# Partial sums of exponentials split between VectorE and GpSimd in the masked cross attentions of a two-layer Perceiver-like block

## The reference

```python
attn = jnp.einsum('bihd,bjhd->bhij', q, k)                 # 512 queries x 8192 keys, 16 heads
attn = jnp.where(padding_mask[:, None, None, :], attn, -jnp.inf)
p = jax.nn.softmax(attn, axis=-1)
ctx = jnp.einsum('bhij,bjhd->bihd', p, v).reshape(b, s1, c)
out = ctx @ Wo.T + bo
```

## Time and profile before

| | us |
|---|---|
| median of 2 runs | 1712.45 (1708.62 to 1716.28) |
| span of the profiled execution | 1710.0 |
| second half of L0x, first to last exponential | about 284 to 442 |
| second half of L1x, first to last exponential | about 1177 to 1354 |
| PE busy | 1608.9 |
| DVE busy | 1028.7 |
| POOL busy | 100.3 |

### The profile page before, as it was taken

How to read it: one execution, slowest core, us unless ns; L and a number is a source line. 1 busy time by engine, 2 the same in 40 slices (tenths; PEclk the granted TensorE clock), 3 DMA queues, 4 the chain that set the end, 5 groups by cost and what they waited for, 6 DMA issues and landing times. The chain is left out here.

```text
span 1710.0 us, 27863 instructions
## 1 busy us (share of the span) xinstructions
PE 1608.9 (94%) x9460; PEld 758.6 (44%) x9471; DVE 1028.7 (60%) x1681; ACT 522.1 (31%) x781; POOL 100.3 (6%) x82
## 2 busy tenths in 40 slices
PE   7999999999899889999999899998999899989997
PEld 3333333222343376666665433332222244467775
DVE  6677777999746551111111599998979945652223
ACT  3434434878413310000000211114658612200000
POOL 0200001000002010000000320000300001010001
PEclk9899998999999989999999999998999999989999
DMA  4442332211067967666661423210412021239996
GB/s 167 149 151 110 143 141 82 64 51 37 0 133 124 197 235 256 235 233 225 235 235 57 152 91 117 74 67 32 158 39 74 0 86 32 100 122 336 325 327 228
DMA packets 73420, 240.28 MB, mean 141 GB/s; under 512 B 7328, under 2 KB 20528, under 8 KB 54032
## 3 DMA queue, kind: packets, MB, share of 16 engines
q1 hardware_dynamic: 64752, 220.42, 39.8%
q10 hardware_dynamic: 6048, 10.69, 1.7%
q0 software_dynamic: 2560, 8.39, 1.5%
HBM read 214.04 MB, written 35.91 MB: 146 GB/s over the span
## 5 line engine op out<-in xcount | busy, mean ns | idle before, releaser
L1564 ACT ACTIVATE BIG<-banks 128x1024 f32<-128x1024 f32 (+5 forms) x320 | 282.1, 934 | 122.5 <-PE banks L1510 121.7
L1086 DVE CUSTOM_DVE_ANT_0 BIG<-banks,MASK,MX 128x512 bf16<-128x512 f32 (+5 forms) x384 | 228.9, 656 | 61.8 <-issue 38.3
L2106 PEld LDWEIGHTS banks<-KF,BIG 128*128 128x128 f32 x1792 | 227.0, 191 | 14.1 <-issue 14.1
L2106 PE MATMUL banks<-KF,BIG 128*128 128x160 f32 (+1 forms) x1792 | 229.2, 289 | 2.6 <-DVE KF L1824 2.0
L2134 PE MATMUL banks<-BIG,PB 128*128 128x512 f32 x448 | 202.9, 600 | 0.0
L695 PE MATMUL banks<-KF,XN 32*128 32x512 f32 (+4 forms) x1280 | 188.8, 609 | 11.4 <-DVE MX L1086 3.8
L1503 PE MATMUL banks<-XN,KF 32*128 32x512 f32 (+4 forms) x1280 | 187.9, 614 | 7.4 <-ACT BIG L1564 5.3
L1615 DVE TENSOR_TENSOR PB<-PB,BIG 128x2048 f32<-128x2048 f32 (+5 forms) x78 | 165.7, 2124 | 22.6 <-ACT BIG L1564 20.2
L1079 DVE TENSOR_REDUCE MXW<-banks 128x2 f32<-128x1024 f32 x128 | 150.3, 1216 | 44.6 <-PE banks L706 43.4
L1470 PE MATMUL banks<-BIG,V 128*32 128x512 f32 (+4 forms) x1280 | 160.4, 570 | 5.0 <-issue 2.6
L2134 PEld LDWEIGHTS banks<-BIG,PB 128*128 128x128 f32 x448 | 81.5, 190 | 113.1 <-issue 112.9
(11 more groups left out here) (296 smaller groups left out, 1468.1 us busy)
## 6 DMA issues: line engine op xcount, KB each, us to landing
BIG<-in_L0f_w SPq DMA_DIRECT2D x64, 1024.0 KB, 4.8
BIG<-in_L1f_w SPq DMA_DIRECT2D x48, 1024.0 KB, 5.7
BIG<-in_mask_q SPq DMA_DIRECT2D x16, 1024.0 KB, 8.0
k_saved<-KF SPq DMA_DIRECT2D x32, 256.0 KB, 2.7
CT<-in_ctx SPq DMA_DIRECT2D x6, 1024.0 KB, 4.8
XNT<-in_ctx SPq DMA_DIRECT2D x6, 1024.0 KB, 6.4
v_saved<-V SPq DMA_DIRECT2D x24, 256.0 KB, 2.4
KF<-k_saved SPq DMA_DIRECT2D x24, 256.0 KB, 3.3
```

Source lines behind the costliest of these rows:

```text
L1086: last = v.tensor_tensor_reduce(m.JUNK[:, 2 * half + e, k0:k1], pair[:, e, k0:k1], bias, 1.0, mx, ALU.add, ALU.max, mx)
L1564: a.activation(m.PE_[:, s % NP, 2 * half:2 * half + 2, q0:q1], m.pair[(2 * s + half) % 3][:, :, q0:q1], ACT.Exp).then_inc(exp_ready, 1)
L2106: last = t.matmul(out, W1[k][:, d, f * P:(f + 1) * P], XE[:, d, :], start=d == 0, stop=d == DC - 1)
```

## The change

In the dynamic attentions alone:

- GpSimd adds tiles 3, 7 and 11 of every block (the last tile of chunks 0, 1 and 2) to `PSUMS[c]` with a `tensor_tensor` of 128 x 2048. It waits for the tile's exponentials and for VectorE's addition before it (`sum_taken` of s - 1), and counts in a semaphore of its own, `pool_summed[c]`. VectorE adds the other thirteen and waits for the three GpSimd semaphores at tile 15. `O.gpsimd`, the four bias additions, stays behind GpSimd's loop in its program.
- The ring has five places. Tiles with s % 4 == 3 take places 3 and 4 in turn, so that each of them is overwritten only eight tiles later; the others stay in places 0 to 2, as before.
- ScalarE's wait for the sum is for VectorE's or GpSimd's count, whichever added the tile that lay there; where that was tile 11 of the block before, it waits for VectorE's tile 15 of that block, which implies it.
- TensorE waits for the three GpSimd semaphores behind its last block.
- The counts of the semaphores and what they are raised by at the start follow from that.

```diff
+    pool_summed = [m.sem(f"{n}_poolsum{c}", dyn) for c in range(DC - 1)]
+    by_pool = [KT_ * c + KT_ - 1 for c in range(DC - 1)] if dyn else []
+    NV = NS - len(by_pool)
+    FAR = 2 * NP
-    B = to_raise(m, dyn, {product_done: NP - 1, sum_taken: NP - 1, added_up: 1})
-    BP, BA = (B + NP - 1, B + 1) if dyn else (0, 0)
+    B = to_raise(m, dyn, {product_done: FAR - 1, sum_taken: NP - 1, added_up: 1})
+    BP, BS, BA = (B + FAR - 1, B + NP - 1, B + 1) if dyn else (0, 0, 0)
-    def tile_free(i, s):
-        return i * NS + s - NP + 1 + BP if dyn else max(0, s - NP + 1)
+    def place(s):
+        return NP if dyn and s % FAR == FAR - 1 else s % NP
+    def before(s):
+        return s - (FAR if dyn and s % NP == NP - 1 else NP)
+    def summed(i, s):
+        return i * NV + sum(x not in by_pool for x in range(s + 1)) + BS
+    def tile_multiplied(i, s):
+        return i * NS + before(s) + 1 + BP if dyn else max(0, s - NP + 1)
+    def tile_summed(act, i, s):
+        if not dyn:
+            act.wait_ge(sum_taken, max(0, s - NP + 1))
+            return
+        last = before(s) % NS
+        back = (before(s) - last) // NS
+        if last not in by_pool:
+            act.wait_ge(sum_taken, summed(i + back, last))
+        elif back == 0:
+            act.wait_ge(pool_summed[last // KT_], i + 1)
+        else:
+            act.wait_ge(sum_taken, summed(i + back, NS - 1))
...
+                if dyn:
+                    with pe.If(i + 1 >= nb):
+                        for sem in pool_summed:
+                            pe.wait_ge(sem, i + 1)
...
         def gpsimd(pool, nb):
+            def body(i):
+                for s in by_pool:
+                    c = s // KT_
+                    wait_alone(pool, exp_ready, (i * NS + s) * 2 + 2 + B)
+                    wait_alone(pool, sum_taken, summed(i, s - 1))
+                    nc.gpsimd.tensor_tensor(m.PSUMS[c], m.PSUMS[c], m.PE_[:, place(s)], ALU.add).then_inc(pool_summed[c], 1)
+            if dyn:
+                active_loop(pool, nb, body)
             O.gpsimd(pool)
...
-                act.wait_ge(product_done, tile_free(i, s))
-                act.wait_ge(sum_taken, tile_free(i, s))
+                act.wait_ge(product_done, tile_multiplied(i, s))
+                tile_summed(act, i, s)
...
-                    dve.wait_ge(exp_ready, (i * NS + s) * 2 + 2 + B)
-                    dve.wait_ge(sum_taken, i * NS + s + BP)
+                    if s not in by_pool:
+                        dve.wait_ge(exp_ready, (i * NS + s) * 2 + 2 + B)
+                        dve.wait_ge(sum_taken, summed(i, s - 1))
+                        if s == NS - 1 and dyn:
+                            for sem in pool_summed:
+                                dve.wait_ge(sem, i + 1)
...
-        m.PE_ = big(0, 4).rearrange("p (b g n) -> p b g n", b=NP, g=G)
+        m.PE_ = big(0, NP + 1).rearrange("p (b g n) -> p b g n", b=NP + 1, g=G)
```

More of the change, by code:

```diff
@@ L1385, in weighted_values @@
     slots_cleared, next_loaded = m.sem(L.name + "_slots", L.fixed == 0), m.sem(L.name + "_next")
-    m.fresh = []
     n = L.name + "_pv"
     dyn = L.fixed is None
+    pool_summed = [m.sem(f"{n}_poolsum{c}", dyn) for c in range(DC - 1)]
+    m.fresh = []
     mask_loaded, bias_ready, sum_zeroed = m.sem(n + "_mask", dyn), m.sem(n + "_bias", dyn), m.sem(n + "_zeroed", L.fixed == 1)
@@ L1470, in times_values @@
                     last = t.matmul(m.bank[6 + c % 2][rows(g), q0:q1], m.V[:, kt[k], HD * h:HD * h + HD],
-                                    m.PE_[:, s % NP, g, q0:q1], start=k == 0, stop=k == KT_ - 1,
+                                    m.PE_[:, place(s), g, q0:q1], start=k == 0, stop=k == KT_ - 1,
                                     skip_group_check=not dyn)
@@ L1537, in tensor @@
             over_blocks(pe, L, nb, body)
-            O.tensor(pe, sum_taken, nb * NS + BP, added_up, nb * DC + BA)
+            O.tensor(pe, sum_taken, nb * NV + BS, added_up, nb * DC + BA)
         @staticmethod
         def gpsimd(pool, nb):
+            def body(i):
[6 more added lines that the diff above has]
+                active_loop(pool, nb, body)
             O.gpsimd(pool)
@@ L1558, in exponentials @@
                 q0, q1 = L.queries_of[kt[k]]
-                act.wait_ge(product_done, tile_free(i, s))
-                act.wait_ge(sum_taken, tile_free(i, s))
+                act.wait_ge(product_done, tile_multiplied(i, s))
+                tile_summed(act, i, s)
                 for half in range(2):
                     act.wait_ge(scores_ready, (i * NS + s) * 2 + half + 1 + B)
-                    a.activation(m.PE_[:, s % NP, 2 * half:2 * half + 2, q0:q1], m.pair[(2 * s + half) % 3][:, :, q0:q1],
+                    a.activation(m.PE_[:, place(s), 2 * half:2 * half + 2, q0:q1], m.pair[(2 * s + half) % 3][:, :, q0:q1],
                                  ACT.Exp).then_inc(exp_ready, 1)
@@ L1607, in body @@
                         dve.wait_ge(sum_zeroed, c + 1)
-                    dve.wait_ge(exp_ready, (i * NS + s) * 2 + 2 + B)
-                    dve.wait_ge(sum_taken, i * NS + s + BP)
                     dst = m.PSUMS[c][:, :, q0:q1]
[L1612 to L1615, removed]
+                    if s not in by_pool:
[4 more added lines that the diff above has]
+                                dve.wait_ge(sem, i + 1)
+                        if k == 0 and (q0, q1) == (0, T) and not dyn:
+                            v.tensor_copy(dst, m.PE_[:, place(s)]).then_inc(sum_taken, 1)
+                        else:
+                            v.tensor_tensor(dst, dst, m.PE_[:, place(s), :, q0:q1], ALU.add).then_inc(sum_taken, 1)
                     if k == 1 and c:
```

## The result

The changed kernel takes 1756.11 us (median of 2 runs, 1754.47 to 1757.74) against 1712.45: 1.0274 times the time before, 95% interval 1.0233 to 1.0315. It is slower, by 43.7 us; 1747 was forecast, with a range of 1730 to 1762.

The account below looks back on a forecast made before the run. TensorE and ScalarE together were taken to set the pace, VectorE close behind. L0x 22.4 plus L1x 12.0 us made +34.4 on the median of 1712.45, so 1747 us, with a range of 1730 to 1762.

Parts of the forecast that it names:

- Bound and headroom: Both cross attentions: TensorE and ScalarE set the pace, 38.9 us a block; taking VectorE's load away entirely gives 1.1 us.
- Turns and H: VectorE beside GpSimd: each waits for the other's whole instruction; H, the time one GpSimd addition keeps VectorE out, is 4.2 us.
- The sum of L0x: Stage L0x: twelve moved additions at 1.88 us, 22.6, less 0.7 and 0.8, plus 1.3 for bias additions: 22.4 us longer.
- the two deductions, 0.7 and 0.8: L0x: 0.7 us of VectorE's waits for exponentials in the first block, 0.8 for mask instructions running during GpSimd's tile 11.
- The sum of L1x: Stage L1x, third and fourth blocks counted: 11.3 less 0.6 of waits plus 1.3 for bias additions, 12.0 us longer.
- The lag is worked off: L1x: VectorE's 5.6 us lag from the first block vanishes in the slower second block, 56.6 us long, costing nothing.
- The ring: L0x from the second block: lag passes the ring's 7 us, ScalarE waits some 5 us a block for VectorE, no extra cost.
- rival 2: Both attentions: one long GpSimd instruction holds VectorE out less than four short ones, 2.85 to 3.5 us; 1723 to 1735; chance 0.14.
- rival 3: Both attentions: GpSimd's tiles cost VectorE nothing and the 1.1 us of the two ends come back; 1711 us; chance 0.05.
- rival 4: Both attentions: TensorE's clock falls in the new stalls, adding 10 to 15 us; about 1760 us; chance 0.08.
- rival 5: Both attentions: GpSimd's instruction is slower still, or GpSimd comes late and ScalarE waits for it; 1755 to 1765; chance 0.05.
- the case that came true: Both attentions: turns as forecast, GpSimd holding VectorE out 3.84 to 4.6 us; 1740 to 1754, likeliest 1747; chance 0.68.

Follow-up runs that it names:

- e1: Changed kernel with GpSimd's three additions a block replaced by one-element fills, those tiles left out of the sums: 1726.3 us, 1.0089 times the kernel before.
- e7: Changed kernel with GpSimd filling 128 x 2048 of unread bf16 in place of its additions, those tiles left out of the sums: 1728.7 us.
- e8: Changed kernel with GpSimd copying each of its tiles to unread bf16 instead of adding it, those tiles left out of the sums: 1730.0 us.
- e9 to e11: Kernel before with the five-place ring, VectorE making all sixteen additions, GpSimd working uselessly beside them: fills 1719.1 us, one-input copies 1748.4, two-input additions 1787.9.
- e4: Changed kernel with VectorE preparing each quarter of the next block's mask ahead of the additions of tiles 12 to 15: 1744.8 us, 1.0189 times the kernel before.
- e3: Changed kernel with GpSimd's four bias additions in front of its loop, not behind it: 1753.6 us, 1.0243 times the kernel before.
- e6: Changed kernel with GpSimd adding each of its tiles by four 128 x 512 instructions, not one of 128 x 2048: 1743.2 us, 1.0171 times the kernel before.

## Why the prediction was right

**Bound and headroom: right.** That TensorE and ScalarE set the pace and that relief is worth about 1.1 us came from the earlier trace rows; the stages of e1, e7 and e8, 1.4 to 3.0 us shorter, are of that size. One reading does not add up: the rest of VectorE's 39.90 us was put down to L1599 at 0.6 and L1591 at 0.26. A block has four of each, 3.4 us, and only 39.90 - 16 x 2.32 = 2.8 are left. The 39.90 itself was read off and stands.

**Turns and H: right.** The trace gave it, and e9 to e11 isolate it. H, taken as 4.2 between 3.84 and 4.6, is 4.1 to 4.2 at VectorE's rows. But of the 24 additions of 6 us and more that were to be seen there are 13: five turns fell on the small mask instruction (4.5 to 5.0 us), and at six VectorE was idle for so much of the turn that its next addition took only 3.35 to 5.02. The Trainium skill ("SBUF — State Buffer", "Who interferes with whom") names GpSimd's reads and not its writes as what collides with a two-input instruction; the traces agree: 1.58 us lost beside a one-input copy, nothing beside a fill. The 4497 ns of the Trainium skill ("GPSIMD Engine Reference", "3.1 Elementwise — side-by-side cycle accounting") stands against 4.54 us here.

**The sum of L0x: right in its main term, 3.0 us short.** The forecast was 45.5 us a block; VectorE's first additions of the blocks lie 45.68 and 45.57 apart. The bias additions at the end cost 0.46 + 0.95 = 1.4 us, where 1.3 was put: the timeline has the last two additions of VectorE at 6.03 together beside the four of GpSimd,

```profile
464.38 6.03 DVE L1665 TENSOR_TENSOR BIG<-BIG 128x2048 f32<-128x2048 f32 x2
461.75 11.01 POOL L1342 TENSOR_TENSOR X<-X,RAROWS 128x512 f32<-128x512 f32 x4
```

and L1372 did not wait. What failed are the two deductions, 0.7 and 0.8. The mask instruction in L0x was to run while GpSimd holds tile 11, having one tile as input; it was held like the additions (4.54 against 0.34). The first block grew by 6.4 us, more than the full 5.6 of three turns, and the last by 7.5, of which 5.6 are turns and 1.4 the bias. The deductions are 1.5 of the 3.0 us and the bias additions 0.1. Most of the other 1.4 stands in two rows of DVE:

```profile
295.96 5.02 DVE L1665 TENSOR_TENSOR PB<-PB,BIG 128x2048 f32<-128x2048 f32 x1 [2.44 <-ACT BIG L1609]
431.83 6.34 DVE L1665 TENSOR_TENSOR PB<-PB,BIG 128x2048 f32<-128x2048 f32 x1 [0.60 <-ACT BIG L1609]
```

In the first block VectorE, with tile 3 taken from it, stood idle until tile 4 was exponentiated and then still had to wait for GpSimd. That turn cost 2.7 us (tile 4's addition ends 19.73 us behind the first exponential, 17.02 before) and not 1.9. In the fourth block it waited 0.60 us for exponentials at the same place.

**The sum of L1x: 5.4 us short, and this is the step that failed.** "The lag is worked off" in the slow second block was said of VectorE, and it is true of VectorE. But TensorE starts that block only when the mask is there, and the mask is in VectorE's queue. The block started 47.9 us behind the first exponential, 44.1 before; since TensorE paces it, these 3.9 us cannot be made good. They are a longer wait for the mask and a slower stretch of TensorE behind it, taken apart under the rivals. e4 takes them away with an edit that spares VectorE nothing. From the third block on it is 95.4 us against 82.1, 13.3 more, where 11.3 - 0.6 + 1.3 = 12.0 were put. The prediction had named who waits for `sum_taken`, not who waits for `bias_ready`, which is queued behind it.

**The ring: right in effect, wrong in the way.** I expected ScalarE to wait some 5 us a block for VectorE's sums. It waits 5.5 in all; mask and `OACC` stop TensorE first. In L0x this changes nothing, since VectorE has no gap behind its first tiles but one of 0.6 us.

**The rivals.** Less hold for a long instruction (rival 2) fell: it was more than four short ones. The free ride (rival 3) fell. TensorE's clock (rival 4) did fall, against what I argued: windows of the changed kernel, L0x, L1x and the stretch around the first boundary of L0x (busy times, then the granted clock):

```profile
281.20:470.40 189.20, 168.68 (x1296) 47.67 (x1290) 179.59 (x80) 125.78 (x133) 83.07 (x15) 0.91 0.15 41
1199.80:1399.90 200.10, 183.04 (x1356) 52.83 (x1354) 172.56 (x80) 125.80 (x133) 77.14 (x15) 0.93 0.21 65
318.00:334.00 16.00, 12.71 (x92) 3.61 (x88) 16.00 (x11) 8.49 (x10) 6.48 (x1) 0.79 0.12 34
```

Before it was 0.97 in both stages. The drop in the third row comes with the 3.29 us in which TensorE waited for the mask, and the eight score matmuls behind it take 2.09 us, as in L0x's first block at the half level of 1.2 GHz, against 1.30 at 2.4 GHz. VectorE is busy for all 16.00 us of that window, and behind the first block it is idle for 0.9 us in all, so in L0x the clock cost less than 1 us. At L1x's first boundary TensorE sets the pace, and there its part can be read off: the same place in the kernel before on PE and ACT, and windows from the first score matmul to the first exponential, changed kernel, then before.

```profile
1218.72 1.14 PE L1503 MATMUL banks<-XN,KF 32*128 32x512 f32 x8 [1.14 <-ACT BIG L1564]
1221.20 1.94 ACT L1564 ACTIVATE BIG<-banks 128x1024 f32<-128x1024 f32 x2 [2.58 <-PE banks L1510]
...
1243.28:1247.77 4.49, 4.49 (x20) 1.16 (x24) 4.49 (x4) 0.00 (x1) 0.00 (x0) 0.50 0.00 0
...
1218.72:1221.20 2.48, 2.48 (x20) 0.83 (x24) 2.48 (x2) 0.00 (x1) 0.00 (x0) 1.00 0.00 0
```

The same matmuls take 4.49 us at a granted clock of 0.50 and 2.48 at 1.00. So the clock has 2.0 us of the longer boundary and the longer wait (3.75 against 1.14) has 2.6; together they are more than the 3.9, because the last exponential of the first block came 0.9 us sooner after the first one. Rival 4 was right for this place, though not in its size. e4, where TensorE waits 0.95 us there and the granted clock is 1.00, takes away both. GpSimd late (rival 5) did not happen in the changed kernel; e3 and e6 show what it looks like.

**How much was luck.** The measured 1756 lies 2 us above the 1740 to 1754 of the case that came true. The range held it because its top, 1762, was set for an H of 4.92, which was not measured; neither the mask's wait nor the clock at the boundary was in the sum. That the change came out slower than 2% was called at 0.51, no better than even.

## What to carry to other kernels

Before work is moved to another engine, look for one place in the trace where the two already run side by side, and read the durations there: a few bias additions foretold this result. An engine that is busy for most of a stage but waited for by nobody has no relief to give, and a second engine whose reads keep it out can turn it into the bound. And when an instruction gets slower, follow every semaphore that its queue still has to raise, small ones (a mask) above all: a stage that seems to have slack may need that one value to start.

## What the runs showed of the hardware that I had not expected

- Instructions of VectorE with one tile as input can be held too. `TENSOR_SCALAR` from uint8 to bf16, 128 x 128, took 4.54 us beside a GpSimd addition and 0.34 elsewhere. The addition to `OACC`, whose second input is PSUM, was never longer than 0.68, also where it lay beside a GpSimd addition (463.78).
- The hold depends on more than the number of columns: 4.2 us for 2048 columns with accumulator and tile, 3.29 for X + X into bf16, 1.58 for a cast copy, 0 for a fill of 1.80 us.
- Behind a wait of TensorE of 3.3 us stood a stretch at the lower level of its clock (0.79 in the mean of 318 to 334), and behind one of 3.75 us another (0.50); in 446 to 480 of the kernel before it idled for 5 us in smaller pieces and the granted clock stayed 1.00. At L1x's boundary it added 2.0 us to the 2.6 of the wait.
